# Loads of expert numbers on TensorE as steps of their own, with the written order of five engines made anew

## The chip, the cores and the metric

The kernel runs on one core of a Trainium2 chip. The metric is the device time of one execution in microseconds. TensorE multiplies matrices, VectorE, ScalarE and GpSimd work on rows, SyncE issues most transfers (DMAs). Each engine takes its instructions in the order in which the program has them, and waits on semaphores where it needs another engine's result.

## The reference

Input x has 16 sequences of 256 tokens of 128 numbers, 4096 tokens. Layer 0 is a quantized linear map, a block with a gated linear recurrence and a gelu feed-forward, and the quantized map again; layer 1 is a mixture of experts, a gated linear attention, and the same mixture again:

```python
x = x + 0.5 * _L0_ffn_ref(_layernorm(x), weight_q, weight_scale, bias)
x = x + _L0_attn_ref(_layernorm(x), norm1_w, Wx, Wy, conv_w, ..., Wg, Wu, Wd)
x = x + 0.5 * _L0_ffn_ref(_layernorm(x), weight_q, weight_scale, bias)
x = x + 0.5 * _L1_ffn_ref(_layernorm(x), Wg_s, Wu_s, Wd_s, Wg, Wu, Wd, Wr, rb)
x = x + _L1_attn_ref(_layernorm(x), Wq, bq, Wk, bk, Wv, bv, Wg, bg, Wo, bo)
x = x + 0.5 * _L1_ffn_ref(_layernorm(x), Wg_s, Wu_s, Wd_s, Wg, Wu, Wd, Wr, rb)
# _L1_ffn_ref: each token goes to its 2 best of 8 experts, and to a shared one
probs = jax.nn.sigmoid(einsum('bsh,eh->bse', x, Wr) + rb)
scores, idx = jax.lax.top_k(probs, 2)
out = shared + sum over e of cw[..., e] * (silu(x @ Wg[e].T) * (x @ Wu[e].T)) @ Wd[e].T
```

## The kernel before

The tokens lie in SBUF as 8 units of 512 (u); two units make a pair. Every operation of a unit is a small function, named by its stage, its work and its engine: q_ is the quantized map, f_ the recurrence, m_ its feed-forward, r_ the routing, e_ the shared expert, x_ and t_ the routed tiles, c_ the collection of their results, g_ the attention, k_ constants. A last argument p is the pass: 0 is the first mixture (and its q_ is the first map), 1 the second. The program of each engine is a list of calls of these functions, written out, some 300 to 750 calls each; a planner made the lists, and semaphores carry the dependences.

Routing. For each unit the tokens' experts are found (r_rank, r_counts, r_slot), and GpSimd scatters each token's row to its expert's region in HBM (r_scatter, rows_by_expert). After 2, 4, 6, 7 and 8 units VectorE writes the next part of two tables (table_vector, one wave each): etab, the expert of each tile of 128 rows, and rtab, its first row. A pass has 71 tiles (NT); the waves begin at tiles 0, 9, 25, 41 and 49.

Tiles. SyncE fetches a tile's rows (t_load_sync, into tin) and its expert's two first matrices (t_weights_sync, into twt, a ring of 4), with row and expert taken from the tables into registers, four entries at a time. TensorE turns the tile (the end of x_io_tensor, L1064), ScalarE copies it to tint, TensorE makes the gate and up products (x_up_tensor, L1083), ScalarE the silu (tsil), VectorE the product thidt (x_hid_vector, L1121), and five tiles later (LAG_DOWN) TensorE makes the down product (x_io_tensor, L1058) from e_dn, which holds all experts' last matrices in SBUF and is addressed by a register. ScalarE scales it (x_out_scalar), GpSimd scatters it to rows_done (t_store_gpsimd). When a unit's tiles are all stored (t_stored_sync), SyncE fetches its two rows per token (c_fetch_sync) and VectorE adds them to x (c_add_vector, L1161 and L1162).

The register for the down product is loaded on TensorE's own queue, by values_of (L1001), in front of the down product of every fourth tile:

```python
if chunk_at(j):
    pe.wait_ge(s_table, WAVES * p + wave_of(j) + 1)
    expert_pe.update(values_of(ENG.PE, etab[p], chunk_at(j), E_ROUTED))
pe.wait_ge(s_thid, g + 1)
```

The start. ScalarE makes constants (k_copies, k_decay), copies the turned quantized rows for TensorE (q_copy_scalar, qit, L446), scales w_sq (k_weights_scalar, L1404), and turns the masks to bytes and scales w_gu (k_masks_scalar, L1407 and L1408). k_weights waits for the five loads of s_load, which SyncE issues behind x:

```python
act.wait_ge(s_load, 16 * LOADS)
```

VectorE adds the product of the quantized map to x (q_out_vector, L462); GpSimd adds the bias (q_bias, L425), takes roots (L339), makes f_apply (L619, into h) and f_b (L589), which VectorE's scan waits for (f_scan, L597); TensorE's f_mix (L307) waits for bufE of that.

## Time and profile before

| | |
|---|---|
| median of 3 runs | 792.85 us (786.53 to 799.07) |
| span of the profiled execution | 692.3 us |
| its own time | not listed; against the median 100.6 us lie around the span |
| TensorE busy | 600.1 us, 87% of the span |
| VectorE, GpSimd, ScalarE busy | 497.2, 419.3, 387.7 us |
| moved by DMA | 100.97 MB |

The span goes from the first to the last instruction. An engine is busy while it computes; waiting, registers and the issue of DMAs don't count. Numbers in brackets in the rows further on are idle time just ahead of an instruction, and what ended it. PE is TensorE's matmul, PEld its weight load, DVE VectorE, ACT ScalarE, POOL GpSimd, SP SyncE.

### The profile page before, as it was taken

Reading aid. Unit: us, or ns where it says so; the run is one execution under the profiler, and the core shown is the slowest. Engines: PE = TensorE matmul, PEld = TensorE weight load, DVE = VectorE, ACT = ScalarE, POOL = GpSimd, SP = SyncE. Lnnn points to the kernel's source line nnn. Section 1 sums busy time; section 2 is a strip of 40 time slices with the busy share of each in tenths; the row PEclk is TensorE's granted clock in tenths of the full one; section 3 lists DMA queues with packets and bytes.
Section 4 is the critical chain, followed back from the end, with each engine's and each line's share of the span. In section 5 each row is a group of like instructions: output and inputs, shape, how many; then the busy total and the mean of one; then the engine's idle time right before and its main releaser. Section 6 shows DMA issues by size and latency. Waiting matters only on the chain.

```text
span 692.3 us, 14370 instructions
## 1 busy us (share of the span) xinstructions
PE 600.1 (87%) x4124; PEld 476.3 (69%) x4124; DVE 497.2 (72%) x1721; ACT 387.7 (56%) x1019; POOL 419.3 (61%) x445
## 2 busy tenths in 40 slices
PE   0366999999989998999897899999999999978974
PEld 0224565655666797888696686769879989857863
DVE  7997999978998865557224798989877766553335
ACT  2395968988766545444353728466565355533541
POOL 5276696488567777567643614553776575775552
PEclk9996999999999999999999999999999999999997
DMA  7999000001033355666768600124216556566796
GB/s 258 410 411 371 0 1 1 1 0 32 13 99 94 97 156 161 186 193 180 211 176 245 235 6 1 35 66 131 74 43 172 153 151 177 161 182 189 231 297 232
DMA packets 60125, 100.97 MB, mean 146 GB/s; under 512 B 10288, under 2 KB 28592, under 8 KB 59792
## 3 DMA queue, kind: packets, MB, share of 16 engines
q1 hardware_dynamic: 50832, 81.52, 38.5%
q0 software_dynamic: 8640, 17.84, 7.4%
q8 instruction: 35, 0.57, 0.4%
q10 hardware_dynamic: 576, 0.69, 0.3%
q14 instruction: 42, 0.34, 0.2%
HBM read 61.79 MB, written 38.23 MB: 144 GB/s over the span
## 4 chain that ended last, share of the span: by engine, by line
PE 43%; DVE 13%; DMA 9%; issue 6%; POOL 3%; SPq 2%; ACT 2%; POOLq 0%; DVEq 0%; ACTq 0%
PE bank L1083 13%; PE bank L1058 6%; PE bank L1296 5%; DMA tin<-rows_by_expert 3%; PE bank L969 3%; PE bank L955 3%; PE bank L944 2%; DMA hid<-rows_done 2%; DMA rows_done<-tout,tdst 2%; PE bank L1064 2%; DMA rows_done<-tout,tin 1%; POOL rows_by_expert L840 1%; DVE qt L417 1%; PE bank L312 1%; PE bank L307 1%
## 5 line engine op out<-in xcount | busy, mean ns | idle before, releaser
L840 POOL DMA_INDIRECT rows_by_expert<-xx,sidx x128 | 128.1, 1001 | 72.2 <-issue 34.0
L1083 PE MATMUL bank<-tint,twt 128*128 128x128 f32 x1136 | 151.8, 282 | 6.0 <-DVE thidt L1121 3.4
L1083 PEld LDWEIGHTS bank<-tint,twt 128*128 128x128 f32 x1136 | 141.1, 196 | 22.0 <-issue 12.3
L1132 POOL DMA_INDIRECT rows_done<-tout,tin x98 | 96.3, 983 | 57.5 <-ACT tout L1107 34.8
L1121 DVE TENSOR_TENSOR thidt<-tsil,bank 128x256 f32<-128x256 f32 x142 | 58.2, 418 | 95.8 <-ACT tsil L1099 74.1
L1099 ACT ACTIVATE tsil<-bank 128x256 f32<-128x256 f32 x142 | 53.9, 384 | 89.9 <-PE bank L1083 88.4
L1058 PE MATMUL bank<-e_dn,thidt 128*128 x568 | 90.6, 286 | 15.5 <-DVE thidt L1121 7.3
L1058 PEld LDWEIGHTS bank<-e_dn,thidt 128*128 128x128 f32 x568 | 76.8, 195 | 25.2 <-issue 24.8
L1107 ACT ACTIVATE tout<-bank,tin 128x128 f32<-128x128 f32 x142 | 50.2, 366 | 62.9 <-PE bank L1064 43.7
L1132 POOL DMA_INDIRECT rows_done<-tout,tdst x44 | 43.7, 993 | 49.0 <-ACT tout L1107 35.9
L1296 PEld LDWEIGHTS bank<-bufA,bufB 128*127 128x127 f32 (+6 forms) x448 | 47.7, 176 | 11.6 <-issue 6.7
L1296 PE MATMUL bank<-bufA,bufB 128*127 128x127 f32 (+6 forms) x448 | 52.2, 263 | 3.7 <-DVE bufA L1272 1.8
L1092 ACT ACTIVATE tint<-bank 128x128 f32<-128x128 f32 x142 | 37.1, 274 | 27.6 <-PE bank L1064 27.3
L1064 PE MATMUL bank<-consts,tin 128*128 128x128 f32 x142 | 39.5, 282 | 6.4 <-DMA tin<-rows_by_expert 6.4
L687 PE MATMUL bank<-ut,w_gu 128*128 128x512 f32 x64 | 34.4, 620 | 1.7 <-DVE hid L696 1.7
L673 PE MATMUL bank<-ut,w_gu 128*128 128x512 f32 x64 | 34.5, 621 | 1.0 <-DVE x L709 1.0
L955 PE MATMUL bank<-xtr,s_gu 128*128 128x512 f32 x64 | 34.0, 614 | 0.9 <-ACT egate L951 0.9
L944 PE MATMUL bank<-xtr,s_gu 128*128 128x512 f32 x64 | 33.3, 603 | 0.4 <-DVE carry L809 0.3
L969 PEld LDWEIGHTS bank<-e_dn,ehid 128*128 128x128 f32 x256 | 30.1, 192 | 3.1 <-DVE ehid L963 1.7
L969 PE MATMUL bank<-e_dn,ehid 128*128 128x128 f32 x256 | 31.4, 276 | 0.8 <-DVE ehid L963 0.8
L963 DVE TENSOR_TENSOR ehid<-egate,bank 128x512 f32<-128x512 f32 x32 | 21.9, 684 | 13.2 <-PE bank L955 8.4
L951 ACT ACTIVATE egate<-bank 128x512 f32<-128x512 f32 x32 | 19.1, 596 | 20.5 <-PE bank L944 20.4
(272 smaller groups left out, 1331.0 us busy)
## 6 DMA issues: line engine op xcount, KB each, us to landing
twt<-moe_gu SPq DMA_DIRECT2D x142, 256.0 KB
rows_by_expert<-tout SPq DMA_DIRECT2D x25, 715.0 KB, 20.0
tin<-rows_by_expert SPq DMA_DIRECT2D x142, 65.0 KB, 2.6
hid<-rows_done SPq DMA_DIRECT2D x12, 512.0 KB, 5.5
x<-x_in SPq DMA_DIRECT2D x8, 256.0 KB, 4.4
rows_by_expert<-xx,sidx POOLq DMA_INDIRECT x128
out<-x SPq DMA_DIRECT2D x8, 256.0 KB, 3.9
rows_done<-tout,tin POOLq DMA_INDIRECT x98
```

Source lines behind the costliest of these rows:

```text
L840: pool.indirect_dma_start(out=rows_by_expert, out_offset=bass.IndirectOffsetOnAxis(ap=sidx[h][:, k:k + 1], axis=0), in_=xx[h][:, r, t, :], ...
L944: pe.matmul(bank[E_BANKS[p]][:, :], s_gu[:, 0, j * P:(j + 1) * P], xtr[u % 2][:, :], start=True, stop=True).then_inc(s_sg, 1)
L955: pe.matmul(bank[E_BANKS[p]][:, :], s_gu[:, 1, j * P:(j + 1) * P], xtr[u % 2][:, :], start=True, stop=True).then_inc(s_su, 1)
L969: m = pe.matmul(bank[E_BANKS[p]][:, t * P:(t + 1) * P], ehid[u % 2][:, j, t * P:(t + 1) * P], e_dn[:, SHARED, j, :], start=(j == 0), stop= ...
L1058: m = pe.matmul(bank[b][:, P:2 * P], thidt[g % TURNS][:, c, :], e_dn[:, expert_pe[j], c, :], start=(c == 0), stop=(c == IJ - 1))
L1064: pe.transpose(bank[b][:, 0:P], tin[g % RING][:, 0:D], ident).then_inc(s_tt, 1)
L1083: m = pe.matmul(bank[UP_BANKS[p][j]][:, c * P:(c + 1) * P], weights[:, c * P:(c + 1) * P], tint[g % TURNS][:, :], start=True, stop=True)
L1099: act.activation(tsil[g % TURNS][:, :], bank[UP_BANKS[p][j]][:, 0:INNER], ACT.Silu).then_inc(s_tsil, 1)
L1107: act.activation(tout[:, g % RING, :], bank[IO_BANKS[p][j + LAG_DOWN]][:, P:2 * P], ACT.Copy, scale=tin[g % RING][:, ROW_SCORE:ROW_SCORE + ...
L1121: dve.tensor_tensor(thidt[g % TURNS][:, :, :].rearrange("p j c -> p (j c)"), tsil[g % TURNS][:, :], bank[UP_BANKS[p][j]][:, INNER:2 * INNE ...
L1132: pool.indirect_dma_start(out=rows_done, out_offset=bass.IndirectOffsetOnAxis(ap=dst, axis=0), in_=tout[:, g % RING, :], in_offset=None).t ...
L1296: m = pe.matmul(gb(u, lv % 2)[0:P - w, c * P + w:(c + 1) * P], bufB[h][:, c * P:(c + 1) * P - w], bufA[h][:, c * P + w:(c + 1) * P], start ...
```

## The change

The register load of TensorE leaves x_io_tensor and becomes a function and a step of its own, with the same wait. All five lists are written in a new order; each of the four other engines has the same calls as before, and TensorE's has the 38 loads as calls.

```diff
+        def x_ids_tensor(pe, p, j):
+            pe.wait_ge(s_table, WAVES * p + wave_of(j) + 1)
+            expert_pe.update(values_of(ENG.PE, etab[p], chunk_at(j), E_ROUTED))
+
         def x_io_tensor(pe, p, s):
...
                 g = p * NT + j
-                if chunk_at(j):
-                    pe.wait_ge(s_table, WAVES * p + wave_of(j) + 1)
-                    expert_pe.update(values_of(ENG.PE, etab[p], chunk_at(j), E_ROUTED))
                 pe.wait_ge(s_thid, g + 1)
```

Of the lists, which make up nearly all of 3300 lines of difference, two lines as an example, from SyncE's:

```diff
-            t_weights_sync(sp_, 0, 0)
-            t_load_sync(sp_, 0, 1)
```

TensorE, the first load of pass 0 before: it stands behind the second product of a shared expert (L955), right ahead of the first down product, whose address is computed from it (ISA).

```order
L1083 MATMUL bank<-tint,twt 128x128 x4
L955 MATMUL bank<-xtr,s_gu 128x512
L1001 TENSOR_LOAD etab
L1058 ISA
L1058 MATMUL bank<-e_dn,thidt 128x128
L1058 ISA
L1058 MATMUL bank<-e_dn,thidt 128x128
```

After: it stands behind a shared expert's first product (L944) and ahead of the turning of the pass's first tile; the first down product comes 30 rows later.

```order
L793 MATMUL bank<-chosen,ones_bf 128x8
L944 MATMUL bank<-xtr,s_gu 128x512
L1001 TENSOR_LOAD etab
L1065 MATMUL bank<-consts,tin 128x128
L1429 MATMUL bank<-a_sq,across 128x128
L1430 MATMUL bank<-a_sq,across 128x128
L673 MATMUL bank<-ut,w_gu 128x512
```

The load moved from the step that needs it to one that doesn't. Others moved by less, and four stand directly behind another load: of tiles 41 and 65 of pass 0, and of tiles 13 and 37 of pass 1 (behind those of tiles 37, 61, 9 and 33). The first load of pass 1 now stands behind the attention's value product of unit 5 and ahead of its step g_diag of unit 4. On VectorE the table of that wave now stands ahead of r_stats of units 3 and 2 and of r_mom of pair 1, and behind g_mom of pair 3.

ScalarE, the start, before: after the constants come both copies of qit, then the scaling of w_sq, then the normalizing of units 0 and 1.

```order
L1400 ACTIVATE sp<-sp 128x1
L446 ACTIVATE qit0<-bank5 128x512
L446 ACTIVATE qit1<-bank5 128x512
L1404 ACTIVATE w_sq<-w_sq,cols 128x256
L355 ACTIVATE tt0<-x,lf_shift,r1 128x128 x4
L355 ACTIVATE tt1<-x,lf_shift,r1 128x128 x4
```

After:

```order
L1401 ACTIVATE sp<-sp 128x1
L1405 ACTIVATE w_sq<-w_sq,cols 128x256
L446 ACTIVATE qit0<-bank5 128x512
L446 ACTIVATE qit1<-bank5 128x512
L1408 ACTIVATE masks<-hid0 128x2048
L1409 ACTIVATE w_gu<-w_gu,cols 128x1024
L355 ACTIVATE tt0<-x,lf_shift,r1 128x128 x4
```

The scaling of w_sq moved ahead of both copies, and the masks and w_gu, which before came behind the third copy, ahead of the normalizing. On GpSimd the root lf_rstd and f_apply of unit 1 moved ahead of the bias of units 2 and 3.

VectorE, the end of the program, before: x_hid (L1121) of tiles 69 and 70 stands between the additions of units 2 and 3 (L1161, L1162), and the shared expert's product (L963) behind the latter.

```order
L1121 TENSOR_TENSOR thidt2<-tsil2,bank2 128x256
L1121 TENSOR_TENSOR thidt3<-tsil3,bank4 128x256
L1161 TENSOR_TENSOR x<-x,hid1 128x512
L1162 TENSOR_TENSOR x<-x,hid1 128x512
L1121 TENSOR_TENSOR thidt0<-tsil0,bank0 128x256
L1121 TENSOR_TENSOR thidt1<-tsil1,bank1 128x256
L1113 TENSOR_TENSOR tdst<-tin9,away_of 128x1
L1161 TENSOR_TENSOR x<-x,hid1 128x512
L1162 TENSOR_TENSOR x<-x,hid1 128x512
L963 TENSOR_TENSOR ehid1<-egate1,bank6 128x512
L1161 TENSOR_TENSOR x<-x,bufA0 128x512
L1162 TENSOR_TENSOR x<-x,bufB0 128x512
```

After, with the same functions one line later:

```order
L1122 TENSOR_TENSOR thidt3<-tsil3,bank4 128x256
L1122 TENSOR_TENSOR thidt0<-tsil0,bank0 128x256
L1122 TENSOR_TENSOR thidt1<-tsil1,bank1 128x256
L1114 TENSOR_TENSOR tdst<-tin9,away_of 128x1
L963 TENSOR_TENSOR ehid1<-egate1,bank6 128x512
L1162 TENSOR_TENSOR x<-x,hid0 128x512
L1163 TENSOR_TENSOR x<-x,hid0 128x512
L1162 TENSOR_TENSOR x<-x,hid0 128x512
L1163 TENSOR_TENSOR x<-x,hid0 128x512
L1162 TENSOR_TENSOR x<-x,hid1 128x512
L1163 TENSOR_TENSOR x<-x,hid1 128x512
L975 SCALAR_TENSOR_TENSOR x<-bank6,x 128x512
```

The additions of units 0, 1 and 2 moved from between the tiles to behind the last tile, and behind the shared expert's product ehid. On TensorE the shared expert's gate product of unit 7 (L944), which stood ahead of the products of tile 65, moved behind the last down product. On SyncE the wait for tile 57's store and the fetches of units 0 to 5 moved behind the weights of tile 70, and all eight stores of x behind the fetch of unit 7.

## Rows read from the trace of the kernel before

**Rows 1.** The page: span, and busy time, share and instructions of each engine
```profile
span 692.3 us, 14370 instructions
...
PE 600.1 (87%) x4124; PEld 476.3 (69%) x4124; DVE 497.2 (72%) x1721; ACT 387.7 (56%) x1019; POOL 419.3 (61%) x445
```

**Rows 2.** Busy time by stretch: PE, PEld, DVE, ACT, POOL, clock, DMA
```profile
0.00:80.00 80.00, 39.67 (x180) 22.64 (x181) 66.84 (x237) 44.48 (x93) 40.98 (x60) 0.91 0.81 313
80.00:600.00 520.00, 491.80 (x3435) 392.57 (x3434) 390.74 (x1362) 309.17 (x814) 329.12 (x336) 0.99 0.37 107
600.00:692.30 92.30, 68.65 (x512) 61.13 (x510) 39.60 (x123) 34.08 (x113) 49.23 (x50) 0.94 0.72 220
```

**Rows 3.** Line 1001, the register loads: ns min/median/max, first, last start
```profile
L1001 PEldq TENSOR_LOAD <-etab x38: 311/1022/1222, 226.0 to 675.9; - x38
```

**Rows 4.** Groups by line: the down products behind those loads
```profile
L1058 PE MATMUL bank<-e_dn,thidt 128*128 x568 | 90.6, 286 | 15.5 <-DVE thidt L1121 7.3 <-issue 3.8 <-ACT tint L1092 2.7
```

**Rows 5.** TensorE in order of time about two loads: start, us, idle before
```profile
377.92 0.71 PE L1058 MATMUL bank<-e_dn,thidt 128*128 x4 [0.93 <-ACT tint L1092]
...
654.62 0.71 PE L1058 MATMUL bank<-e_dn,thidt 128*128 x4 [0.44 <-issue]
```

**Rows 6.** ScalarE in order of time, 17 to 41 us
```profile
17.70 0.60 ACT L446 ACTIVATE qit<-bank 128x512 bf16<-128x512 bf16 x1 [8.49 <-PE bank L312]
...
23.00 0.50 ACT L1404 ACTIVATE w_sq<-w_sq,cols 128x256 f32<-128x256 f32 x1
30.17 3.19 ACT L355 ACTIVATE tt<-x,lf_shift,r 128x128 f32<-128x128 f32 x8 [6.67 <-POOL lf_shift L351]
...
38.12 1.91 ACT L1407 ACTIVATE masks<-hid 128x2048 uint8<-128x2048 int32 x1
39.92 1.15 ACT L1408 ACTIVATE w_gu<-w_gu,cols 128x1024 f32<-128x1024 f32 x1
```

**Rows 7.** SyncE issuing the last load of s_load; DMA issues: us to landing
```profile
11.56 0.72 SPq L1451 DMA_DIRECT2D w_r<-moe_r  x1
...
w_r<-moe_r SPq DMA_DIRECT2D x1, 4.0 KB, 8.6
```

**Rows 8.** TensorE and VectorE in order of time, 18 to 55 us
```profile
18.44 1.44 PE L454 MATMUL bank<-wq_bf,qit 128*128 128x128 bf16 x12 [0.78 <-ACT qit L446]
...
20.63 1.11 DVE L462 SCALAR_TENSOR_TENSOR x<-bank,qs,x 128x128 f32<-128x128 f32 x4
...
54.42 1.27 DVE L597 TENSOR_TENSOR_SCAN bufE<-bufA,bufB 128x256 f32<-128x256 f32 x2 [3.06 <-POOL bufB L589]
```

**Rows 9.** GpSimd in order of time, 36 to 54 us
```profile
42.57 1.27 POOL L425 TENSOR_TENSOR x<-x,half_qb 128x512 f32<-128x512 f32 x1 [3.37 <-DVE qt L417]
43.79 1.83 POOL L339 TENSOR_TENSOR lf_rstd<-lf_ve,neg_half 128x8 f32<-128x8 f32 x1
45.73 7.43 POOL L619 TENSOR_SCALAR h<-x,lf_mean,lf_rstd 128x128 f32<-128x128 f32 x8
```

**Rows 10.** Waits of 0 to 80 us: who for whom, us, times, longest
```profile
PE bank L307 <- DVE bufE L605: 5.8, 1, 5.8
```

**Rows 11.** All engines in order of time, the last 30 us
```profile
666.26 0.71 PE L1058 MATMUL bank<-e_dn,thidt 128*128 x4 [1.50 <-DVE thidt L1121]
...
672.13 0.69 DVE L1161 TENSOR_TENSOR x<-x,hid 128x512 f32<-128x512 f32 x1 [5.45 <-DMA hid<-rows_done]
...
674.26 2.07 PE L1058 MATMUL bank<-e_dn,thidt 128*128 x8 [3.01 <-DVE thidt L1121]
...
679.49 1.02 PE L955 MATMUL bank<-xtr,s_gu 128*128 128x512 f32 x2
...
688.41 0.69 DVE L1161 TENSOR_TENSOR x<-x,bufC 128x512 f32<-128x512 f32 x1 [2.53 <-DMA bufD<-rows_done]
```

**Rows 12.** The table of pass 1 wave 0; TensorE at that time
```profile
466.83 0.23 DVE L895 SCALAR_TENSOR_TENSOR rtab<-stab,base,consts 128x9 int32<-128x9 f32 x1
...
467.23 1.05 PE L1247 MATMUL bank<-w_vo,xc 128*128 128x128 f32 x8
```

More of the change, by code:

```diff
@@ L2041, in _ @@
[L2041 to L2045 removed]
+            for j in range(51, 55):
                 x_hid_vector(dve, 0, j)
@@ L3182, in _ @@
                 x_io_tensor(pe, 1, j)
-            for j in range(59, 62):
+            for j in range(59, 61):
                 x_up_tensor(pe, 1, j)
@@ L3775, in _ @@
+            g_late_scalar(act, 6, 6)
+            for j in range(23, 25):
+                x_in_scalar(act, 1, j)
             for j in range(18, 20):
@@ L3881, in _ @@
+            for j in range(52, 54):
                 x_silu_scalar(act, 1, j)
```

2061 lines of the change are left out of this document (1043 added, 1018 removed).

## The prediction

> **What bounds the kernel now.** I read the busy time by stretch first. TensorE is busy 600.1 us of a span of 692.3 us [rows 1]. Its 92.2 us of idleness lie unevenly: 40.3 us in the first 80 us, 28.2 us in the 520 us that follow, 23.7 us in the last 92.3 us [rows 2]. So from 80 to 600 us the kernel is a TensorE queue, 95% full, and whatever is made new there in the order of the other four engines can only close or open some of 28 us. The two ends are different. At the start VectorE is the fullest engine (66.8 of 80 us) and hands to GpSimd and ScalarE in turn; at the end a chain of stores, fetches and additions closes the span [rows 2]. Second, I read line 1001, the loads of expert numbers: 38 of them on TensorE, median 1.02 us, 0.31 to 1.22 us [rows 3]. That is 38.8 us of its queue, but its sequencer runs a little ahead of the array, so the idle time that a load leaves is shorter: 0.44 us where it stood behind 24 queued matmuls, and 0.93 us where a wait had emptied the queue, a gap that the trace puts down to ScalarE's copy [rows 5]. Third, for the ends, the engines in order of time.
>
> **How the sum is made.** No time is listed for the profiled execution itself; the median of the three runs is 792.85 us, so 100.6 us lie around the span of 692.3 us (94.2 to 106.8 us against the lowest and highest run). I change the span and leave the 100.6 us alone.
>
> **Part 1, the loads.** None is added or removed: 38 before, 38 after, four entries each, with the same wait on s_table. What changes is the place: before, each stood right ahead of the down products that need it; now it stands up to some tens of steps earlier, ahead of a step that doesn't need it. The queue stops for a load all the same. The most that can be won is therefore the idle time ahead of the down products, 15.5 us over all 142 tiles, and of that 7.3 us wait for VectorE's thidt, 3.8 us are put down to nothing (the load behind queued work) and 2.7 us to ScalarE [rows 4]. The most that can be lost is what would happen if no load had cover: 38 x 1.02 = 38.8 us, less the 15.5 us, 23.3 us. Between them I count: the 3.8 and 2.7 us, 6.5 us, may go, because a load that isn't needed yet can sit where the queue is full, and no down product then finds its number missing. Against that, four loads now stand directly behind another load (tiles 37 and 41, 61 and 65 of pass 0; 9 and 13, 33 and 37 of pass 1); the cover is used up by the first, so these cost 4 x 1.02 = 4.1 us. Net: **-2.4 us**, bounds -15.5 and +23.3. The SyncE loads of the same tables, on its own queue, keep their places ahead of the DMAs.
>
> Against a trace with 0.44 us of idleness behind 24 queued matmuls [rows 5] stands a rule. The Trainium skill (TensorE: Matmul & The Clock Gate, "Architectural detail: the array is 16× 32×32, not 1× 128×128") gives TensorE an engine queue of 64 instructions. If so much work were queued, a load of about a microsecond would vanish wherever it stood, and the term would be 0 in place of -2.4 us. The gap of 0.44 us behind 24 matmuls says that the sequencer is less than a load ahead, so the rule doesn't decide here; it is one reason for the case "no effect" below.
>
> **Part 2, the start (0 to 60 us).** Two moves pull against each other. ScalarE's k_weights moves ahead of both copies of qit. It waits for five loads, of which w_r is the last: issued at 11.56 us, 8.6 us to landing, so 20.2 us [rows 7]. Before, the first copy ran at 17.70 us, and k_weights at 23.00 us found its data there [rows 6]. Now the copy stands behind it: 20.2 + 0.50 (k_weights) + 0.60 (copy) + 0.14 (18.44 - 17.70 - 0.60, to the first matmul) + 1.44 (the quantized product) = 22.9 us, where VectorE read that product at 20.63 us [rows 6, 8]. That is +2.3 us on the chain of units 0 and 1, whose 12 to 20 us have no other cover, VectorE having been full there. For it speaks that k_masks (1.91 + 1.15 us), which ran at 38.12 us just ahead of unit 0's tanh, now sits in ScalarE's idle 6.67 us before its normalizing at 30.17 us [rows 6]: -3.1 us there. And GpSimd takes lf_rstd and the first f_apply (1.83 us and half of 7.43 us, 5.5 us) ahead of q_bias 2 and 3, into holes such as the 3.37 us before 42.57 us; before, both stood between 43.79 us and the product f_b.0, for which VectorE's scan at 54.42 us waited 3.06 us [rows 8, 9] and, behind it, TensorE 5.8 us [rows 10]. With the delay: f_b.0 comes 5.5 - 2.3 = 3.2 us earlier, if the square root comes as early, for which the delay of 2.3 and the gain of 3.1 us leave only 0.8 us. I take the middle: **-2.0 us**, bounds +2.3 (the delay alone) and -5.5 (GpSimd's move alone). TensorE then starts its full stretch so much earlier.
>
> **Part 3, the end (660 to 692 us).** Before, VectorE's additions of units 0, 1 and 2 stood ahead of x_hid of tiles 64 to 69, and each pair waits for a fetch: 5.45 us at 672.13 us. TensorE waited for thidt 1.50 us at 666.26 us and 3.01 us at 674.26 us [rows 11]. Now all eight additions stand behind x_hid of tile 70, and SyncE issues the fetches behind the last weights. The 4.5 us go, and so does the gate product of unit 7 (0.9 us, by the step from 679.49 us to the down products, one 512-wide product of two records), which moves behind the last tile. TensorE's tile work so ends 5.4 us earlier, at 674.1 us and not 679.5 us. What is late next: VectorE. From the end of tile work: gate 0.9, silu 0.7, up 0.9, product 0.7 and hand-overs 0.2 make 3.4 us, because the product ehid now stands ahead of the additions; then 8 additions of two halves of 0.69 us, 11.1 us, the shared addition 0.7 us; then the last store. Before, from the same point, 12.8 us passed to the end of the span, of which 2.5 us are that store (688.41 + 2 x 0.69 = 689.8 to 692.3) [rows 1, 11]. Now: 3.4 + 11.1 + 0.7 + 2.5 = 17.7 us, 4.9 us more. Net: **-0.5 us**, bounds -5.4 (the additions hide) and +4.9 (no stall goes). The fetch of unit 7, which closed the span with 2.53 us of waiting [rows 11], is no longer last.
>
> **Part 4, the rest.** The order of all five engines from 60 to 660 us is new, mostly by shifts of under ten steps. No wait of the trace can be assigned to a shift; with 28.2 us of idleness in 520 us I take 0, bounds -5 and +5 (a sixth of it). The hand-over near 376 to 396 us has the same shape on both sides: two additions, statistics, then tiles.
>
> Sum: -2.4 - 2.0 - 0.5 + 0 = -4.9 us, a span of 687.4 us and a time of **788.0 us**.
>
> **The rivals.**
> *No effect.* The queue stops for 1.02 us wherever a load stands, pairs cost what covered ones win, and start and end cancel. For it: a gap under half a microsecond per load [rows 5], and that loads keep their number. Time: 792.9 us.
> *The start runs late.* The 2.3 us of delay stay, GpSimd's move doesn't help since the square root is the later one, and the clock costs something: the granted clock means 0.91 over the first 80 us [rows 2], so 7.2 us are lost to it in a stretch where TensorE idled for 5.8 us at a time [rows 10]; a longer idleness there may cost a third more, 2.4 us. With the end as bad as +0.5 us: 792.9 + 5.2 = 798 us.
> *TensorE held at a table* (slower). An early load brings the wait on s_table forward, and all matmuls queue behind it, the attention's too. The tightest place is the first load of pass 1: its table was finished at 467.1 us, and the load now stands behind the value product at 467.23 us and the next gate product, so it is reached at about 469 us [rows 12]. It decides from 2 us: if VectorE comes to the table 5 us later in respect of TensorE, the queue stands for 3 us, and with the same at four of the ten waves 12 us are lost: 805 us. Against it: VectorE's order now has that table ahead of three steps (two statistics and r_mom of pair 1) that stood before it, and behind one (g_mom of pair 3).
> *More idleness closed.* A planner's new order that knows the stops places everything better. Half of the 23.7 us of the last stretch beside the sum: -11.8 - 4.4, 777 us. Against it: the end's gain is given back by VectorE, as worked out.
>
> **How the numbers follow.** Forecast 0.40, no effect 0.17, start late 0.18, held at a table 0.12, more closed 0.13. The predicted time is 788.0 us. The range reaches from the case with more idleness closed, 777 us, nearly to the one held at a table, 803 us; the bounds of part 1 that lie outside need every load bare or every gap shut. What a measurement of this kernel can tell from no change is about 2%, 15.9 us: below 777.0 us I see 0.08 (part of "more closed"), above 808.7 us 0.08 (a table hold worse than priced, or many bare loads), between them 0.84.
>
> **What would show it.** Right: TensorE's idle time ahead of the down products falls from 15.5 us to about 9 us, and no weight load has a microsecond of "issue" but behind a pair of loads; ScalarE's first qit copy starts near 20.7 us; VectorE's scan comes before 53 us; the last x_hid isn't delayed by a fetch; the last eight additions run back to back up to the end. Wrong: if the first copy stays at 15 to 18 us (the five loads were there), if the additions' fetches land so late that VectorE waits between them, or if a load's wait for its table shows as idleness of many microseconds.

## The result, and the profile after

The changed kernel took 806.07 us (median of four runs, 805.42 to 809.94) beside 795.32 us of the kernel before (median of four runs, 786.53 to 799.07). The ratio of the two is 1.0178, with a 95% interval of 1.0105 to 1.0252. The change is slower by 10.75 us between the medians and by 14 us by the ratio, which is less than the 2% that a measurement of this kernel was said to tell. The forecast was 788.0 us, a gain, in a range of 777 to 803 us: both the sign and the range missed.

The page of the changed kernel, with the lines that answer to [rows 1] and [rows 4], and one line of VectorE for later (the multiplications of the gated attention's levels):

```profile
span 804.6 us, 14372 instructions
PE 628.8 (78%) x4124; PEld 497.9 (62%) x4124; DVE 511.1 (64%) x1721; ACT 384.6 (48%) x1019; POOL 413.9 (51%) x445
L1059 PE MATMUL bank<-e_dn,thidt 128*128 x568 | 93.2, 292 | 23.5 <-issue 9.6
L1314 DVE TENSOR_TENSOR bufA<-bufA,tseg 128x256 f32<-128x256 f32 x56 | 30.6, 547 | 15.5 <-remote 7.6
```

A span of 804.6 us stands beside a time of 806.42 us: 1.8 us lie around it, not the 100.6 us that the prediction took from [rows 1] and the median. The profile before must come from an execution unlike the timed ones, an eighth shorter. Most likely it ran on another chip: its mean granted clock is 0.972, as in the quick executions of experiment 1 (0.97 to 0.98), against 0.931 in the changed kernel's first profile. So neither [rows 1] and 792.85 us nor these two profiles may be set side by side. Experiments 1 and 2 ran both kernels on one quick chip. Their windows, in the columns of [rows 2], first the kernel before, then the changed one:

```profile
0.00:80.00 80.00, 41.35 (x186) 23.33 (x187) 68.04 (x240) 45.26 (x94) 41.25 (x61) 0.91 0.81 313
80.00:600.00 520.00, 496.01 (x3496) 397.88 (x3494) 395.71 (x1388) 313.62 (x829) 335.38 (x342) 0.99 0.38 109
600.00:681.10 81.10, 60.30 (x445) 52.85 (x445) 34.04 (x96) 29.18 (x97) 42.22 (x43) 0.94 0.75 234
```
```profile
0.00:80.00 80.00, 38.71 (x180) 21.47 (x180) 67.97 (x234) 44.66 (x93) 41.45 (x62) 0.94 0.81 313
80.00:600.00 520.00, 487.85 (x3402) 389.11 (x3402) 399.71 (x1362) 307.89 (x813) 321.96 (x332) 0.99 0.36 106
600.00:694.30 94.30, 70.90 (x544) 64.03 (x542) 41.31 (x127) 34.75 (x115) 50.08 (x52) 0.91 0.73 222
```

In the changed kernel TensorE does 2.6 us less work in the first 80 us and 8.2 us less in the next 520. It is 10.8 us behind at 600 us, and pays for it at the end (70.90 against 60.30 us). One figure in the middle row gives the hint: VectorE is busy 4.0 us longer, with 26 instructions fewer. Over the whole span it is busy 509.0 us against 497.8, for the same 1721 instructions. Nothing was added to its work; its instructions took longer.

### The profile page after: what moved, and what is told of

Same layout as the page of the kernel before. It is cut to its first block, busy times and chain, and to the rows that moved or that the text cites. A ratio compares the mean times of both kernels' runs of the same rounds, so it can differ in the third digit from the quotient of the medians.

```text
span 804.6 us, 14372 instructions
## 1 busy us (share of the span) xinstructions
PE 628.8 (78%) x4124; PEld 497.9 (62%) x4124; DVE 511.1 (64%) x1721; ACT 384.6 (48%) x1019; POOL 413.9 (51%) x445
## 2 busy tenths in 40 slices
DMA packets 60125, 100.97 MB, mean 125 GB/s; under 512 B 10288, under 2 KB 28592, under 8 KB 59792
## 4 chain that ended last, share of the span: by engine, by line
PE 48%; DVE 19%; another core or an unknown queue 13%; issue 9%; ACT 6%; DMA 3%; SPq 1%; POOL 1%; ACTq 0%; DVEq 0%; POOLq 0%
PE bank L1084 13%; PE bank L1059 6%; PE bank L1297 3%; PE bank L673 2%; PE bank L307 2%; PE bank L944 2%; PE bank L312 2%; PE bank L687 2%; PE bank L969 2%; PE bank L955 2%; PE bank L1065 2%; DVE qt L417 2%; PE bank L702 1%; DVE thidt L1122 1%
## 5 line engine op out<-in xcount | busy, mean ns | idle before, releaser
L1084 PE MATMUL bank<-tint,twt 128*128 128x128 f32 x1136 | 163.8, 296 | 50.9 <-DVE thidt L1122 36.7
L1084 PEld LDWEIGHTS bank<-tint,twt 128*128 128x128 f32 x1136 | 150.3, 208 | 65.9 <-DVE thidt L1122 43.9
L1059 PE MATMUL bank<-e_dn,thidt 128*128 x568 | 93.2, 292 | 23.5 <-issue 9.6
L1059 PEld LDWEIGHTS bank<-e_dn,thidt 128*128 128x128 f32 x568 | 80.2, 202 | 39.1 <-issue 38.9
L1297 PE MATMUL bank<-bufA,bufB 128*127 128x127 f32 (+6 forms) x448 | 55.4, 271 | 17.4 <-DVE at L1326 10.9
L1297 PEld LDWEIGHTS bank<-bufA,bufB 128*127 128x127 f32 (+6 forms) x448 | 50.1, 183 | 25.8 <-DVE tseg L1319 16.1
L1314 DVE TENSOR_TENSOR bufA<-bufA,tseg 128x256 f32<-128x256 f32 x56 | 30.6, 547 | 15.5 <-remote 7.6
L955 PE MATMUL bank<-xtr,s_gu 128*128 128x512 f32 x64 | 35.3, 635 | 2.1 <-ACT egate L951 2.1
L969 PE MATMUL bank<-e_dn,ehid 128*128 128x128 f32 x256 | 34.8, 294 | 1.0 <-DVE ehid L963 1.0
L969 PEld LDWEIGHTS bank<-e_dn,ehid 128*128 128x128 f32 x256 | 33.3, 209 | 3.0 <-DVE ehid L963 2.6
L944 PE MATMUL bank<-xtr,s_gu 128*128 128x512 f32 x64 | 34.1, 615 | 0.6 <-DVE ehid L963 0.6
L963 DVE TENSOR_TENSOR ehid<-egate,bank 128x512 f32<-128x512 f32 x32 | 21.8, 682 | 18.3 <-PE bank L955 9.3
```

The source lines that it names most:

```text
L955: pe.matmul(bank[E_BANKS[p]][:, :], s_gu[:, 1, j * P:(j + 1) * P], xtr[u % 2][:, :], start=True, stop=True).then_inc(s_su, 1)
L969: m = pe.matmul(bank[E_BANKS[p]][:, t * P:(t + 1) * P], ehid[u % 2][:, j, t * P:(t + 1) * P], e_dn[:, SHARED, j, :], start=(j == 0), stop= ...
L1059: m = pe.matmul(bank[b][:, P:2 * P], thidt[g % TURNS][:, c, :], e_dn[:, expert_pe[j], c, :], start=(c == 0), stop=(c == IJ - 1))
L1084: m = pe.matmul(bank[UP_BANKS[p][j]][:, c * P:(c + 1) * P], weights[:, c * P:(c + 1) * P], tint[g % TURNS][:, :], start=True, stop=True)
L1297: m = pe.matmul(gb(u, lv % 2)[0:P - w, c * P + w:(c + 1) * P], bufB[h][:, c * P:(c + 1) * P - w], bufA[h][:, c * P + w:(c + 1) * P], start ...
```

## The experiments

All ratios are to the kernel before, timed on the same chip beside the experiment. The chips differ: for experiments 1 to 12 (three chips) that kernel took 684 to 686 us, for 13 to 18 (two others) it took 796 to 799 us, about as with the first result. The changed kernel itself was timed with the first result (1.0178) and in experiment 2 (1.0167). Together these give 1.017, give or take 0.005, an estimate from the two intervals. Where 5 to 12 are compared with its 696.0 us, the microseconds are across chips and good to some 3 or 4 us, so the ratios are what counts.

**1 and 2. Both kernels again.** No edit.

> The kernel before, once more, for its span. The changed kernel's four executions took 805.4 to 809.9 us at spans of 803.6 to 808.1, so under 2 us lie around its span; the profiled execution of the kernel before had 792.85 beside a span of 692.3. If the start or the end of the kernel before lies outside the span by its nature, its span is again near 692 and its clock near 0.97. If that profile is of an execution unlike the timed ones, the span is now 785 to 797, within 2 us of the time, at a clock near 0.93, and TensorE's idle time in it is nearer to 150 us (the changed kernel) than to 66 us (the profile before).

> The changed kernel again, on the same chip as the next two and the kernel before: 1.3% (1.0 to 2.0%) over the kernel before, as the first comparison had it.

The kernel before took 684.5 us (684.11 in the runs beside it), with a span of 681.1 us in its profiled execution. The changed kernel took 696.0 us, with a span of 694.3 us: a ratio of 1.0167 (1.0094 to 1.0240). The slowdown is the same on the quick chip, 12 us, and under 2 us lie around either span. What the expectation took for typical of the kernel, a span of 785 to 797 us, is what a slower chip gives.

**3 and 4. The loads of expert numbers.** In 3 they go back into x_io in the changed order; in 4 they are separate in the order before.

```diff
 (3)  -            x_ids_tensor(pe, 0, 0)          and 37 more
      +                if chunk_at(j):
      +                    pe.wait_ge(s_table, WAVES * p + wave_of(j) + 1)
      +                    expert_pe.update(values_of(ENG.PE, etab[p], chunk_at(j), E_ROUTED))
 (4)  the reverse, in the kernel before
```

> The changed kernel with the loads of expert numbers back inside the step that needs them; every other step in the order of the changed kernel. If the separate loads cost the time (TensorE waits at them for tables, or a load of four registers behind another costs about 1 us each), this is 8 to 13 us faster than the changed kernel, 793 to 798 us. If the order of the other steps costs it, it is within 3 us of the changed kernel; by my own forecast of the loads' worth (2.4 us) it is 0 to 3 us slower than the changed kernel, 806 to 809.

> The kernel before with the loads alone as steps of their own, each as many steps ahead of its first use as in the changed kernel (or as many as the tile's table allows); no other step moves. If the loads cost the time, it is 8 to 13 us slower than the kernel before (803 to 808). If the order does, it is within 3 us of the kernel before; by my forecast 2.4 us faster (793).

3 took 700.2 us, ratio 1.0237 (1.0173 to 1.0300): 4.2 us slower than the changed kernel. The two intervals overlap, but all four runs of 3 (699.28 to 702.20 us) lie above all four of the changed kernel (692.32 to 698.82 us) on the same chip. 4 took 690.5 us, ratio 1.0101 (1.0025 to 1.0177): 6 us slower than before. So early loads helped in one order and hurt in the other. TensorE's groups by line, in the columns of [rows 4], of the changed kernel and of experiment 3:

```profile
L1059 PE MATMUL bank<-e_dn,thidt 128*128 x568 | 88.7, 283 | 6.8 <-DVE thidt L1122 2.4 <-ACT tint L1093 2.0 <-issue 1.7
```
```profile
L1058 PE MATMUL bank<-e_dn,thidt 128*128 x568 | 89.8, 284 | 13.4 <-issue 7.6 <-DVE thidt L1121 3.3 <-ACT tint L1092 1.6
```

The part put down to nothing ("issue") falls from 7.6 to 1.7 us: a load right ahead of its use leaves the array idle, an early one mostly doesn't. Experiment 4 has seven pairs of loads standing directly behind each other, the changed kernel four. Here is one of the seven, in TensorE's weight loads in order of time; the two register loads themselves (at 340.03 and 341.18 us) have no row in this view:

```profile
340.03 0.14 PEld L1065 LDWEIGHTS bank<-consts,tin 128*128 128x128 f32 x1 [1.19 <-DMA tin<-rows_by_expert]
342.43 0.93 PEld L1059 LDWEIGHTS bank<-e_dn,thidt 128*128 128x128 f32 x4 [2.26 <-issue]
```

Weight loads stood still for 2.26 us at two loads in a row. The matmuls behind the seven pairs waited 0.4 to 2.1 us each, 8.4 us together, and those behind the changed kernel's four pairs 0.2 to 1.1 us, 2.2 us together. That the separate loads make the loss (8 to 13 us) is out. The new order costs 16 us with the loads inside (700.2 against 684.1 us) and 5.5 us with them early in both (696.0 against 690.5 us), though experiment 4 has three more pairs.

**5, 6, 7 and 8. Where in time.** Each list is cut where its steps begin in the trace: up to the cut one kernel's order, behind it the other's. 5, 6 and 7 begin as the kernel before, to 150, 345 and 520 us; 8 begins as the changed one, to 150 us. The lines for ScalarE in 5 (against the changed kernel), as an example:

```diff
-            k_weights_scalar(act)
             q_copy_scalar(act, 0, 0)
             q_copy_scalar(act, 1, 0)
-            k_masks_scalar(act)
+            k_weights_scalar(act)
             f_norm_scalar(act, 0)
...
```

> The order of the kernel before for every step that it has begun by 150 us of its span, on all five engines, and from there the order of the changed kernel. If what the changed kernel's start loses on TensorE (17.06 against 13.75 us to the first matmul, but 6.5 and 7.9 us of waits behind the first transposes; 4.5 us less matmul time done by 150 us) stays lost to the end, this is 3 to 5 us faster than the changed kernel's 696 us, 691 to 693. If it is absorbed before the second table, which ends at 221.0 us in the kernel before and at 220.6 in the changed one, it is within 2 us of 696.

> The order of the kernel before to 345 us, then that of the changed kernel. In the traces the changed kernel falls a further 2 us behind in TensorE's finished work between 240 and 320 us, and its down products of tile 35 end 7 us later. If the losses add up by stage: 689 to 691 us. If what counts is only the table of pass 1 (458.1 against 465.1 us) and its cause lies before 345 us: 687 to 689. If neither: the same as the cut at 150 us.

> The order of the kernel before to 520 us, then that of the changed kernel. Between 345 and 520 us the changed kernel falls 6 us further behind in TensorE's finished work, with waits of 2.81 us at 435.7 and 2.08 us at 494.9 for VectorE's level steps, and ends the second table of pass 1 at 520.2 us against 503.1. If the losses add up by stage, 685 to 688 us: only the changed end is left, worth 2 to 3 us over the kernel before's 684. If the start or the middle is no cause, it stays near the figure of the cut at 345 us.

> The mirror of the cut at 150 us: the changed kernel's order to 150 us, then that of the kernel before (with the loads inside the step, as there). If the changed start costs 3 to 5 us that are never won back, 687 to 689 us against 684. If it is absorbed, within 2 us of 684.

They took 690.95, 693.1, 687.2 and 687.7 us, at ratios of 1.0095 (1.0063 to 1.0127), 1.0126 (1.0086 to 1.0166), 1.0043 (1.0013 to 1.0073) and 1.0041 (1.0017 to 1.0066). The start costs 5.0 us when it is taken away (5, against 696.0) and 3.7 us when it is put in (8). The stretch from 150 to 345 us costs nothing (2 us the other way, within what two such figures tell). From 345 to 520 us it is 5.9 us, clear of the intervals. Behind 520 us some 3 us are left.

**What the trace shows at those places.** VectorE and then GpSimd in the changed kernel, in order of time:

```profile
433.52 0.72 DVE L1326 COPY_PREDICATED at<-masks,bank 128x256 f32<-128x256 uint8 x1
434.06 3.18 DVE L1314 TENSOR_TENSOR bufA<-bufA,tseg 128x256 f32<-128x256 f32 x1
437.16 0.41 DVE L1316 TENSOR_TENSOR bufB<-bufB,tseg 128x256 f32<-128x256 f32 x1
...
493.56 3.31 DVE L1316 TENSOR_TENSOR bufB<-bufB,tseg 128x256 f32<-128x256 f32 x1
```
```profile
434.45 2.49 POOL L1195 TENSOR_TENSOR x<-x,rows 128x512 f32<-128x512 f32 x2
```

A multiplication of 0.41 us takes 3.18 us while GpSimd adds the output bias to two units in a row (2.49 us). The one at 493.56 us does the same, beside another such pair (494.09 us, 2.49 us). Behind the first TensorE waits, since the next level needs it:

```profile
438.55 1.58 PE L1297 MATMUL bank<-bufA,bufB 128*124 128x124 f32 x8 [2.81 <-DVE at L1326]
```

I then took, for each VectorE instruction of either trace, its time over the median of its line and tile, and summed what exceeds it by over 0.25 us. I call this sum the excess. It is 14.2 us, in 13 instructions, in the kernel before (experiment 1), and 27.9 us, in 28, in the changed one (experiment 2). By stretch the changed kernel has 6.3 us more up to 150 us, 3.2 more from there to 345, and 4.1 more from 345 to 520 us. All but one of the 28 overlap a GpSimd addition, product or scaling of a tile. The excess is 13.7 us more beside a span that is 13.2 us longer, but that the two figures agree is chance: the 3.2 us between 150 and 345 us cost no time (experiments 5 and 6).

**9 and 10. GpSimd busy, but reading nothing.** In the changed kernel (9) and the one before (10) the 24 bias additions become memsets of about the same length, so the biases are missing from the result. Each memset first waits for the one before it to end (left out of the lines shown).

```diff
-            pool.tensor_tensor(xg(u), xg(u), half_qb[...].to_broadcast(...), ALU.add).then_inc(s_qxb, 1)
+            pool.memset(junk[:, :], 0).then_inc(s_qxb, 1)
-            pool.tensor_tensor(xg(u), xg(u), rows[:, None, R_BO:...].to_broadcast(...), ALU.add).then_inc(s_xbo, 1)
+            pool.memset(junk[:, :], 0).then_inc(s_xbo, 1)
```

> The changed kernel with its 24 additions of a bias on GpSimd (quantized layer L425, 16 times; gated layer L1194, 8 times) replaced by a memset of about the same length into a spare tensor: GpSimd stays busy as long, but reads nothing from SBUF; the biases are left out of the result. Theory P (port): a GpSimd instruction that reads SBUF stops a VectorE instruction with two SBUF inputs until it ends. VectorE then has none of its level multiplications at 3.2 or 3.3 us (0.42 us instead), the instructions stretched by over 0.25 us go from 28 with 27.9 us of excess to about 15 with under 12, and the kernel is 6 to 11 us faster than the changed kernel, 685 to 690 us. Rival O (order alone: the steps' places cost the time, the stretched instructions are by-play): within 2 us of 696.

> The kernel before with the same replacement of the 24 bias additions by memsets that read nothing; the biases are left out of the result. In its trace 13 instructions are stretched, by 14.2 us in all, 10 us of it beside these additions, but only some on the path. Theory P: 2 to 6 us faster than before (678 to 682), so that the distance between the two kernels, 12 us, shrinks to 5 to 8. Rival O: 684, and the distance stays 12.

9 took 684.6 us, ratio 0.9982 (0.9952 to 1.0013); 10 took 681.7 us, ratio 0.9963 (0.9932 to 0.9993). Some 11 us go from the changed kernel (13 by the ratios) and 2.5 us from the one before. Of the 12 us between the two 2.9 us are left, 1.3 by the ratios, which can't be told from zero. Both kernels still run the same 4124 matmuls and move the same 100.97 MB, so a change in which experts the tokens go to, which the missing biases can bring, leaves the amount of work as it was. The same place in experiment 9, GpSimd and then VectorE:

```profile
432.64 2.68 POOL L1205 MEMSET junk<- 128x1408 uint8 x2
```
```profile
432.62 0.42 DVE L1326 TENSOR_TENSOR bufB<-bufB,tseg 128x256 f32<-128x256 f32 x1
432.95 0.29 DVE L1329 TENSOR_TENSOR tseg<-tseg 128x128 f32<-128x128 f32 x1
...
434.30 0.42 DVE L1324 TENSOR_TENSOR bufA<-bufA,tseg 128x256 f32<-128x256 f32 x1
434.63 0.43 DVE L1326 TENSOR_TENSOR bufB<-bufB,tseg 128x256 f32<-128x256 f32 x1
```

GpSimd is busy for 2.7 us beside them, and no multiplication is longer than 0.44 us. Over the gated layer that line has min/median/max 410/425/472 ns here:

```profile
L1324 DVE TENSOR_TENSOR bufA<-bufA,tseg x37: 410/425/472, 400.6 to 518.1; 128x256 f32<-128x256 f32 x37
```

against 405/424/3181 ns in the changed kernel:

```profile
L1314 DVE TENSOR_TENSOR bufA<-bufA,tseg x38: 405/424/3181, 399.6 to 503.0; 128x256 f32<-128x256 f32 x38
```

The time comes back where these stretched instructions stood. Counted in the traces, TensorE's 1900th matmul ends at 354.3 us in the changed kernel and at 354.1 in experiment 9, its 2900th at 512.1 and at 502.4 us (498.4 in the kernel before). So nearly 10 of the 11 us come back in between. Up to 150 us nothing comes back: TensorE is busy 104.5 us there in the changed kernel, 103.7 in experiment 9 and 109.3 in the kernel before.

The Trainium skill (SBUF — State Buffer, "Who interferes with whom") states this rule: a VectorE instruction with two inputs in SBUF contends with a GpSimd instruction that reads SBUF, not with one that only writes it. Traces and rule agree, 3.18 against 0.42 us. The same page of the Trainium skill says under "SBUF: two separate sides" that whoever starts first gets the port pair and the other blocks; here VectorE's row begins 0.39 us ahead of GpSimd's and VectorE is the one that waits. GpSimd's recorded start is rough, so this doesn't refute it, but the starts of rows can't be used to tell who will block.

What I expected of the excess did not come: it fell from 27.9 us only to 20.9 us, in 23 instructions, and not to under 12. Of what is left 9.9 us lie before 150 us, where it was 10.4. Some of it stands beside GpSimd's other additions, which still read, and some beside the memsets: VectorE's tensor_scalar instructions of the quantized layer are still stretched there, one to 0.91 us where the median of its line is 0.43. The Trainium skill (SBUF — State Buffer, "Who interferes with whom") counts tensor_scalar among the instructions that can take both port pairs and then contend with any GpSimd instruction, and the trace agrees. In order of time, VectorE and GpSimd of experiment 9:

```profile
18.08 0.91 DVE L437 TENSOR_SCALAR qi<-qt 128x512 bf16<-128x512 f32 x1
```
```profile
17.43 1.27 POOL L430 MEMSET junk<- 128x1408 uint8 x1 [0.71 <-DVE qt L419]
```

**11. One cast, later.**

```diff
-            k_weights_scalar(act)
             q_copy_scalar(act, 0, 0)
             q_copy_scalar(act, 1, 0)
+            k_weights_scalar(act)
```

> The changed kernel with one step moved: ScalarE's cast of the router weights (k_weights) behind its first two copies of turned tokens, as in the kernel before. In the changed kernel's trace the cast ends at 20.22 us, and the first copy at 20.70 against 18.27, the first normalization of the gated layer ends 2.4 us later, its first scan starts 1.2 us later. If that wait makes the loss of the start (3.7 to 5.0 us by the cuts at 150 us): 691 to 693 us. If it is only the delay of the scan: 1.2 us, 694.8. If the port makes it: within 1 us of 696.

It took 689.6 us, ratio 1.0071 (1.0038 to 1.0105): 6.4 us faster than the changed kernel, and more than any of the three cases gave the step. ScalarE in the changed kernel and then in experiment 11, in order of time:

```profile
19.71 0.51 ACT L1405 ACTIVATE w_sq<-w_sq,cols 128x256 f32<-128x256 f32 x1 [10.58 <-DMA w_r<-moe_r]
20.13 0.58 ACT L446 ACTIVATE qit<-bank 128x512 bf16<-128x512 bf16 x1
```
```profile
14.44 0.60 ACT L446 ACTIVATE qit<-bank 128x512 bf16<-128x512 bf16 x1 [5.26 <-PE bank L312]
21.09 0.60 ACT L446 ACTIVATE qit<-bank 128x512 bf16<-128x512 bf16 x1 [6.06 <-PE bank L312]
21.59 0.50 ACT L1405 ACTIVATE w_sq<-w_sq,cols 128x256 f32<-128x256 f32 x1
```

The changed order of VectorE had brought the first turned tokens 3.3 us forward (TensorE's first matmul at 13.75 us, 17.06 before); the copy would have run at 14.44 us. The cast of 0.5 us, waiting for w_r, held it to 20.13 us. So the step cost 5.7 us at the copy, not the 2.4 us seen against the order before. With the cast out of the way the first scan runs at 51.93 us, 3.5 us ahead of the changed kernel's and 2.3 us ahead of that of the kernel before:

```profile
51.93 1.27 DVE L597 TENSOR_TENSOR_SCAN bufE<-bufA,bufB 128x256 f32<-128x256 f32 x2
```

**12. The end.** The changed kernel to 640 us, then the order before, with VectorE's additions c_add between the last tiles:

```diff
-            for u in range(0, 3): c_add_vector(dve, u, 1)     behind e_hid_vector(dve, 7, 1, 1)
+            c_add_vector(dve, 0, 1)     behind x_dst 67,  c_add_vector(dve, 1, 1)     behind x_hid 66, ...
```

> The changed kernel's order to 640 us, then that of the kernel before for the last 50: VectorE's eight closing additions stand between its last tiles again and not behind them all. In the changed kernel's trace they run from 680.5 to 691.8 us in one row, while in that of before the last of them alone, 677.2 to 678.6, is left after the last load. If that row costs the difference of the two ends (17.2 against 12.9 us after the last down product): 4 us faster than the changed kernel, 692. If the additions in between hold up the last tiles in turn: within 1 us of 696.

It took 697.9 us, ratio 1.0181 (1.0132 to 1.0229): no gain. VectorE in the changed kernel does its additions in one row (first and last of the row):

```profile
680.50 0.69 DVE L1162 TENSOR_TENSOR x<-x,hid 128x512 f32<-128x512 f32 x1
...
691.12 0.69 DVE L1163 TENSOR_TENSOR x<-x,bufD 128x512 f32<-128x512 f32 x1
```

and in experiment 12 it stands in between for a fetch, as in [rows 11]:

```profile
676.34 0.69 DVE L1165 TENSOR_TENSOR x<-x,hid 128x512 f32<-128x512 f32 x1 [6.48 <-DMA hid<-rows_done]
```

What one form of the end saves, the other costs. With experiment 7 this puts the last 3 us between 520 and 640 us, as far as such small figures can be added.

**13, 14 and 16. Moving the bias additions.** In 13 six of GpSimd's eight output-bias steps move in its list; 14 also has the cast of 11; 16 is 5 with the six moves.

```diff
+            g_bias_gpsimd(pool, 2)
+            g_bias_gpsimd(pool, 3)
             r_scatter_gpsimd(pool, 0, 1, 0)
-            g_bias_gpsimd(pool, 2)
-            g_bias_gpsimd(pool, 3)
 ...   4, 5 to behind r_scatter 1.1.3;   6, 7 to behind r_scatter 3.1.3
```

> The changed kernel, computing all of its result, with six GpSimd steps moved in GpSimd's list and nothing else: the bias additions g_bias 2 and 3 ahead of the first scatter of unit 0 (some 17 us earlier, where VectorE's next instructions are statistics with one input), 4 and 5 behind the scatters of unit 1, 6 and 7 behind those of unit 3. Theory P (port): the level multiplications of 3.18, 1.89 and 3.31 us go back to 0.42; TensorE's waits of 2.8 us at 436 and 2.1 us at 495 are gone; 4 to 7 us faster than the changed kernel, 689 to 692. Rival: the gain of the write-only kernel came from leaving work out: within 2 us of 696.

> The changed kernel with those six steps moved and ScalarE's cast of the router weights behind its first two copies. If the two losses are separate (6.4 us by the cast alone, 4 to 7 by the biases), 683 to 686 us, the kernel before's time or a little below it. If they are one and the same shift of phase, 689.

> The order of the kernel before to 150 us, the changed kernel's behind it, with the six bias steps moved. The cut at 150 us alone took 691 us. With 4 to 7 us from the biases: 684 to 687; a version that beats both kernels would be under 682.

These ran on a slower chip. They took 819.0, 814.1 and 811.3 us beside 796.0, at ratios of 1.0290 (1.0240 to 1.0340), 1.0221 (1.0166 to 1.0277) and 1.0190 (1.0139 to 1.0240). The moves repaired nothing: 13 is above the 1.0167 and 1.0178 of the changed kernel, and 16 above the 1.0095 of experiment 5. The cast again gave 5 us (13 to 14), though by the intervals alone that could be nothing. One thing that went wrong is in the trace of 13, VectorE and GpSimd:

```profile
593.59 2.76 DVE L895 SCALAR_TENSOR_TENSOR rtab<-stab,base,consts 128x16 int32<-128x16 f32 x1
```
```profile
593.80 2.50 POOL L1195 TENSOR_TENSOR x<-x,rows 128x512 f32<-128x512 f32 x2
```

The pair now met the table on which all tiles of a wave wait. I had placed the pairs by the trace of another order, and all four were again pairs. This doesn't explain the time, however. The excess in the trace of 13 is 28.5 us, no more than the 30.0 us of the changed kernel's first trace, while 13 is some 1.2% slower. What costs that is open.

**15. Loads one by one.** The kernel before, each load 1 to 5 steps early behind an up product, never two together (two loads stay where they were):

```diff
             x_up_tensor(pe, 0, 36)
+            x_ids_tensor(pe, 0, 33)
```

> The kernel before with the loads as steps of their own, 1 to 5 steps ahead of their use, each behind an up product and never two in a row. The earlier kernel with early loads had eight of them in pairs, and TensorE stood 1.4 to 2.3 us at such a pair. If pairs made that kernel's 6 us: 681 to 684 us, no slower than before. If any early load costs (it shuts the weight loads behind it for 1 us wherever it stands): 688 to 691.

It took 792.75 us beside 795.98, ratio 0.9953 (0.9918 to 0.9987): the one version with the full result that came out faster than the kernel before, by 0.5%. It fits that pairs made the loss of experiment 4. It doesn't show it alone, since the loads also stand nearer to their use and nearly all behind an up product, and it ran on a slower chip than experiment 4.

**17 and 18. GpSimd's whole list swapped.**

```diff
 (17)  @block.gpsimd of the kernel before in the changed kernel
 (18)  @block.gpsimd of the changed kernel in the kernel before
```

> The changed kernel with the whole GpSimd list of the kernel before; the other four lists are the changed kernel's. Moving six bias additions in pairs brought nothing (2.9% over the kernel before, the changed kernel 1.7%), but its trace shows the pairs only met other VectorE instructions: 3.05 us at a level multiplication, 2.7 at a moment, 2.75 at the table. In the list of before, additions 2, 3, 4 and 5 stand singly with other work between them. Theory P (a pair stops VectorE for 2.5 to 2.9 us, a single one for 1.06 at most): fewer stretched instructions over 2 us than the changed kernel's 3 or 4, and 0.4 to 1.0% faster than it, at 1.007 to 1.013 of the kernel before. If the GpSimd list's order has no part: 1.017.

> The mirror: the kernel before with the changed kernel's GpSimd list. Theory P: the pairs 2 and 3, 5 and 6 stand together again, stretched instructions over 2 us return in the gated layer, and it is 0.4 to 1.0% slower than the kernel before. If GpSimd's order has no part: within 0.3%.

17 took 840.9 us beside 798.6, ratio 1.0525 (1.0500 to 1.0549); 18 took 805.4 us, ratio 1.0087 (1.0056 to 1.0118). 18 is as the port theory had it: the excess rises to 23.5 us, and a level multiplication takes 3.19 us:

```profile
486.88 3.19 DVE L1313 TENSOR_TENSOR bufA<-bufA,tseg 128x256 f32<-128x256 f32 x1
```

17 refutes the use that I made of it. Its excess is down to 15.7 us, and it is the slowest of all. TensorE has done 7.5 us less work than in the changed kernel's first trace by 180 us, and 14 us less by 540 us. The trace shows where the first part goes. GpSimd waits 6.32 us for VectorE's xx in front of unit 0's scatters. f_b of unit 6, which the changed kernel has ahead of these scatters, stands behind them and behind two bias additions, though VectorE began to write its input at 165.89 us. VectorE's scan waits 7.68 us for it, and TensorE 6.68 us behind that. GpSimd, VectorE and TensorE of experiment 17, in order of time:

```profile
166.98 1.22 POOL L840 DMA_INDIRECT rows_by_expert<-xx,sidx  x1 [6.32 <-DVE xx L819]
...
174.46 1.25 POOL L589 TENSOR_TENSOR bufB<-bufD,bufB 128x512 f32<-128x512 f32 x1
```
```profile
175.75 1.27 DVE L597 TENSOR_TENSOR_SCAN bufE<-bufA,bufB 128x256 f32<-128x256 f32 x2 [7.68 <-POOL bufB L589]
```
```profile
178.66 0.59 PE L312 MATMUL bank<-ident_bf,qi 128*128 128x128 bf16 x4 [6.68 <-DVE x L462]
```

In all, the scans of 17 wait 10.7 us for f_b; those of the changed kernel never do. The rest of the 3.5% over the changed kernel is not isolated. So the excess is no measure of an order by itself, and 17, which puts such waits in, is no test of the port.

## Why the prediction was wrong

**The base.** "100.6 us lie around the span" is false: 1.75 to 1.9 us do, in every run of these kernels. I should have taken the gap between span and time as a sign that profile and times didn't belong together. The error drops out of the difference of the two kernels, but not out of the reading: the 28.2 us of idleness were those of a quick chip.

**Part 1, the loads, -2.4 us.** The sign and the mechanism held: -4.2 us (experiments 2 and 3). I had the idle time ahead of the down products fall from 15.5 to about 9 us; it fell from 13.4 to 6.8 us. The 4 x 1.02 us for pairs was the right fear, but came to half: the matmuls behind the four pairs waited 2.2 us (experiment 2), though one pair of experiment 4 stopped the weight loads for 2.26 us. The Trainium skill (TensorE: Matmul & The Clock Gate, "Architectural detail: the array is 16× 32×32, not 1× 128×128") gives TensorE a queue of 64 instructions; if that much work always stood ahead of a load, its place would cost nothing. The runs disagree with this use of it: 4.2 us for early loads, and 2.26 us at a pair.

**Part 2, the start, -2.0 us: the first step that failed.** Measured +5.0 and +3.7 us (experiments 5 and 8). The cast's wait itself was read rightly: the copy was forecast to start near 20.7 us and started at 20.13, the product was forecast for 22.9 and VectorE read it at 22.33 us. What failed is its price of +2.3 us. I compared with the copy of before at 17.70 us, and not with the 14.44 us that the changed order would have had: 5.7 us at the copy, and 6.4 us of time when the cast moved back (experiment 11). The gain of 5.5 us on GpSimd did not come through to the scan either: "VectorE's scan comes before 53 us" was wrong, it came at 55.46 us, 54.25 in the kernel before (experiment 1). GpSimd and VectorE in the changed kernel:

```profile
51.94 1.26 POOL L589 TENSOR_TENSOR bufB<-bufD,bufB 128x512 f32<-128x512 f32 x1 [2.06 <-DVE bufB L582]
```
```profile
52.49 0.99 DVE L432 TENSOR_SCALAR qi<-qt 128x512 bf16<-128x512 f32 x1
53.40 1.23 DVE L328 TENSOR_TENSOR lf_msum<-lf_stats 128x8 f32<-128x8 f32 x1
...
55.46 1.27 DVE L597 TENSOR_TENSOR_SCAN bufE<-bufA,bufB 128x256 f32<-128x256 f32 x2
```

GpSimd was free for f_b.0 by 49.9 us, 3.1 us earlier than before (52.96 in experiment 1), but then waited 2.06 us for VectorE's bufB. So f_b.0 came only 1.0 us earlier than before (51.94 us). Then q_bias 4 stood right behind it at 53.16 us, and VectorE, stopped twice for 1.6 us together, was late for the scan by itself. The path that I had through GpSimd ran through VectorE.

**Part 3, the end, -0.5 us.** Experiment 12 doesn't contradict it: with the old end put back the changed kernel takes 1.9 us more, which with intervals of 0.5 and 0.7% to either side can't be told from zero. The picture (the last additions back to back up to the end, no fetch ahead of an x_hid) was right; from TensorE's last down product of a tile the end took 17.2 us for my 17.7, but 12.9 in the kernel before (experiments 2 and 1).

**Part 4, the rest, 0: the second step that failed.** I put at nothing what holds the other half of the loss: 5.9 us between 345 and 520 us (experiments 6 and 7), and some 3 us behind 520 that I can't place. "No wait of the trace can be assigned to a shift" was the wrong question. The trace of before held the mechanism not as a wait but as a duration. VectorE and GpSimd there, in order of time; the first is one instruction of a line whose median is 152 ns:

```profile
390.83 2.57 DVE L1113 TENSOR_TENSOR tdst<-tin,away_of 128x1 int32<-128x1 int32 x1
```
```profile
390.86 2.52 POOL L1194 TENSOR_TENSOR x<-x,rows 128x512 f32<-128x512 f32 x2
```

I had read VectorE's rows by their starts and waits, never by the spread of their lengths, though [rows 9] has GpSimd's additions.

**The rivals.** "Start runs late" (798 us, chance 0.18) had the right place and sign. Its 4.7 us for the start (2.3 of delay, 2.4 of clock) come near the measured 3.7 to 5.0 us, but half of that is luck: the granted clock of the first 80 us rose, from 0.91 to 0.94, where the rival had it cost more. "No effect" (0.17) and "more idleness closed" (0.13) did not come. "TensorE held at a table" (0.12) didn't happen where it was to: the first load of pass 1 ran at 465.99 us, its table was done at 465.1 us, and TensorE shows no idleness there. At the next table it came near: the table was done at 520.21 us, 17 us later than before, and the load for it ran at 520.25 us, but TensorE idled only 0.23 us there. The mechanism that doubled the loss was in no rival.

**What stays open.** The 11 us of experiment 9 go when GpSimd reads nothing at the biases, and most come back where the stretched instructions stood, between 354 and 512 us. That they would be had back by an order of steps alone is not shown: three attempts (13, 16, 17) failed. Experiment 9 gives 11 us and experiment 11 gives 6 us, together more than the 12 us of the change, so the two are not separate shares of it. They were not run together. The 3 us behind 520 us, the loss of 13 and most of the loss of 17 are not explained.

## What to carry to other kernels

Before predicting a new order, list VectorE's instructions that take much longer than others of their line and tile, and see what GpSimd does beside them: here a two-input VectorE instruction stood for as long as GpSimd read, about 1 to 1.6 us with one addition of 128x512 and mostly 2.6 to 3.3 us with two in a row. An order that puts two such steps together next to a serial chain of VectorE can cost what no wait shows. But the sum of such stretches is no forecast of the time, and moving a step in one engine's in-order list can put it behind a longer wait, as in experiment 17. When a step is moved ahead of another, price it against where the other would now be, not where it was. In these kernels a register load on TensorE did best when placed early, behind queued matmuls, and not next to another one.

## What the runs showed of the hardware

The same program took 684 to 686 us on three chips and 796 to 799 us on two others, 16% more, and the ratio of the two kernels was the same (1.0167 and 1.0178). The mean granted clock of the kernel before was about 0.98 on the former and 0.92 on the latter, but a lower clock is the smaller part of it. In the changed kernel's two traces TensorE is busy 628.8 against 597.5 us, 31 of the 110 us; the rest is idleness. The slower executions lose next to nothing up to 190 us (the first table ends at 186.7 us for 185.3). From then on several engines stand at the same time for 4 to 10 us, again and again. Both ScalarE and VectorE in the trace of the changed kernel's first run, in order of time, released together by something that the profile calls remote, while TensorE waits for VectorE:

```profile
221.12 0.60 ACT L680 ACTIVATE gate<-bank 128x512 f32<-128x512 f32 x1 [4.24 <-remote]
221.15 1.13 DVE L462 SCALAR_TENSOR_TENSOR x<-bank,qs,x 128x128 f32<-128x128 f32 x4 [5.63 <-remote]
...
222.42 0.59 PE L312 MATMUL bank<-ident_bf,qi 128*128 128x128 bf16 x4 [4.55 <-DVE x L462]
```

In the table of waits of that run they sum up at one line alone to:

```profile
ACT tsil L1100 <- remote: 52.8, 13, 9.6
```

The traces of experiments 1, 2 and 9, on quick chips, have no such releaser at all. Neither kernel has another core to wait for, and the cause stays open.
